# Channel attention of a decoder layer: products of weights and values in two runs of eight per group of heads in place of four runs of four

## The reference, cut to what matters

```python
x = x + _L0_xattn_ref(_layernorm(x, axis=-1), ctx_2048, ctx_2048)   # the stage changed

def _L0_xattn_ref(q, k, v):                  # 8 heads, d = c = 128, m = n = 512
    qh = q.reshape(b * h, d // h, m)
    kh = k.reshape(b * h, d // h, -1)
    vh = v.reshape(b * h, c // h, -1)
    qk = jnp.einsum('bdm,bdn->bmn', qh, kh) * scale
    sm = jax.nn.softmax(qk, axis=-1)
    ret = jnp.einsum('bmn,bcn->bcm', sm, vh)
    return ret.reshape(b, c, m)
```

## Time and profile before

| | |
|---|---|
| median of three runs | 4041.53 us |
| profiled execution | 4037.83 us, span 4036.0 us |
| PE busy | 3624.9 us (90%) |
| DVE busy | 2861.6 us (71%) |
| ACT busy | 2582.2 us (64%) |
| POOL busy | 1597.4 us (40%) |
| mean granted clock of TensorE | 0.972 |
| ring matmuls L336 | 2048 records, 382 ns each |
| max matmuls L354 | 2048 records, 385 ns each |
| pv matmuls L365 | 4096 records, 604 ns each |
| reductions L302 | 1024, 1219 ns each |
| exponentials L380 | 2048, 602 ns each |

### The profile page before, as it was taken

How to read it: one execution, slowest core, us unless ns; L and a number is a source line. 1 busy time by engine, 2 the same in 40 slices (tenths; PEclk the granted TensorE clock), 3 DMA queues, 4 the chain that set the end, 5 groups by cost and what they waited for, 6 DMA issues and landing times. The chain is left out here.

```text
span 4036.0 us, 86194 instructions
## 1 busy us (share of the span) xinstructions
PE 3624.9 (90%) x24451; PEld 1808.3 (45%) x24451; DVE 2861.6 (71%) x4477; ACT 2582.2 (64%) x6419; POOL 1597.4 (40%) x2090
## 2 busy tenths in 40 slices
PE   5999999999999996699999799999976988889896
PEld 1222222222222221577778544444444654655563
DVE  5888888888888885577777577777764455444545
ACT  2777777777777775577777577777762534445353
POOL 6444444444444440666666122222221242332323
PEclk9999999999999998799999999999998999999998
DMA  7777777777777762333333133333323030120202
GB/s 113 125 120 125 120 125 120 125 120 124 120 125 121 123 107 72 103 113 113 112 113 115 58 93 93 93 94 94 94 74 110 1 126 2 64 65 33 95 1 79
DMA packets 342550, 385.82 MB, mean 96 GB/s; under 512 B 58432, under 2 KB 223040, under 8 KB 342336
## 3 DMA queue, kind: packets, MB, share of 16 engines
q1 hardware_dynamic: 315712, 348.69, 40.2%
q10 hardware_dynamic: 26624, 34.63, 3.3%
HBM read 196.52 MB, written 84.93 MB: 70 GB/s over the span
## 5 line engine op out<-in xcount | busy, mean ns | idle before, releaser
L302 DVE TENSOR_REDUCE a_neg_max<-a_max_ps 128x2 f32<-128x1024 f32 x1024 | 1201.3, 1219 | 195.3 <-PE a_max_ps L354 171.2
L380 ACT ACTIVATE a_P<-a_ring_ps 128x512 f32<-128x512 f32 x2048 | 1084.3, 602 | 382.4 <-PE a_ring_ps L336 379.4
L354 PE MATMUL a_max_ps<-a_K,a_Q 96*128 96x512 bf16 x2048 | 621.2, 385 | 44.0 <-DMA a_K<-a_k_split 39.8
L336 PE MATMUL a_ring_ps<-a_Q,a_K 98*128 98x512 bf16 x2048 | 617.6, 382 | 6.3 <-DMA a_Q<-a_max_rows 4.1
L365 PE MATMUL a_pv_ps<-a_P,a_V 128*32 128x512 f32 x4096 | 544.9, 604 | 1.8 <-ACT a_out_sb L385 1.8
L336 PEld LDWEIGHTS a_ring_ps<-a_Q,a_K 98*128 98x128 bf16 x2048 | 159.1, 96 | 660.2 <-ACT a_P L380 585.3
L1163 ACT ACTIVATE c_P<-c_s_ps,c_bias 128x128 f32<-128x128 f32 x1024 | 362.2, 368 | 137.8 <-DVE c_bias L1035 128.6
L1092 PE MATMUL c_s_ps<-c_KD,c_qT 128*128 128x512 f32 x512 | 276.0, 621 | 33.4 <-ACT c_qT L1154 28.9
L1031 DVE TENSOR_REDUCE c_neg_max<-c_s_ps 128x4 f32<-128x512 f32 x256 | 175.5, 686 | 162.2 <-PE c_s_ps L1093 162.2
L354 PEld LDWEIGHTS a_max_ps<-a_K,a_Q 96*128 96x128 bf16 x2048 | 183.1, 98 | 220.7 <-issue 42.5
L256 POOL TENSOR_SCALAR a_var_eps<-a_mean_var 128x1 f32<-128x1 f32 x64 | 12.2, 191 | 648.4 <-DVE a_mean_var L318 648.1
(11 more groups left out here) (250 smaller groups left out, 7245.3 us busy)
## 6 DMA issues: line engine op xcount, KB each, us to landing
a_Q<-a_q_split SPq DMA_DIRECT2D x384, 128.0 KB
a_K<-a_k_split SPq DMA_DIRECT2D x384, 128.0 KB
heads_out<-a_out_sb ACTq DMA_DIRECT2D x128, 256.0 KB, 2.3
a_x_in<-in_x_dram SPq DMA_DIRECT2D x64, 256.0 KB, 3.6
a_c_in<-in_ctx_dram SPq DMA_DIRECT2D x64, 256.0 KB
a_cT_in<-in_ctxT_dram SPq DMA_DIRECT2D x64, 256.0 KB
b_x_in<-in_x_dram SPq DMA_DIRECT2D x64, 256.0 KB, 2.8
b_o_in<-heads_out SPq DMA_DIRECT2D x64, 256.0 KB
```

The costliest lines, as they stand in the source:

```text
L302: dve.tensor_reduce(neg_max[:, p, 2 * u:2 * u + 2], max_ps[u % 2][:, :, :], AX.X, ALU.max, negate=True).then_inc(max_taken, 1)
L336: pe.matmul(ring(s, use_of(k))[:, :], K[i][:, h, n:n + 128], Q[i][:, h, :], start=True, stop=True).then_inc(scores_filled, 1)
L354: last = pe.matmul(max_ps[u % 2][:, j, :], Q[i][0:KROW, h, m:m + 128], K[i][0:KROW, h, :], start=True, stop=True)
L380: act.activation(P[p][k // NT][:, k % NT, :], ring(s, use_of(k))[:, :], ACT.Exp, scale=SCALE).then_inc(exp_done, 1)
```

## The change

In PE's step function the pv matmuls came behind k = 3, 7, 11 and 15, four each time (one position tile t for four heads). Now they come behind k = 7 and k = 15, eight each time (two position tiles). The semaphore `pv_done` still goes up once per position tile. The waits ahead of the first pv matmul of a group (`exp_done`, `v_done`, `out_copied`) move from k = 3 to k = 7. Nothing else is changed.

```diff
-                    if s.exists(-1) and k % NT == NT - 1:
-
-                        g, i, p, t = s.group(-1), s.slot(-1), s.half(-1), k // NT
-                        if t == 0:
+                    if s.exists(-1) and k % 8 == 7:
+
+                        g, i, p = s.group(-1), s.slot(-1), s.half(-1)
+                        if k == 7:
                             pe.wait_ge(exp_done, g * SCORES + SCORES)
                             pe.wait_ge(v_done, s.batch(-1) + 1)
                             at_least(pe, out_copied, g)
-                        for j in range(G):
-                            last = pe.matmul(pv_ps[32 * j:32 * j + 32, :], V[i][:, t, p * G + j, :], P[p][j][:, t, :],
-                                             start=(t == 0), stop=(t == NT - 1))
-                        last.then_inc(pv_done, 1)
+                        for t in range(k // 8 * 2, k // 8 * 2 + 2):
+                            for j in range(G):
+                                last = pe.matmul(pv_ps[32 * j:32 * j + 32, :], V[i][:, t, p * G + j, :], P[p][j][:, t, :],
+                                                 start=(t == 0), stop=(t == NT - 1))
+                            last.then_inc(pv_done, 1)
```

## The result

The changed kernel takes 4108.58 us (median of four runs, 4107.43 to 4110.64), the kernel before in the same comparison 4040.68. The ratio is 1.0168, with a 95% interval of 1.015 to 1.0185: 68 us slower. The forecast was 4118, slower.

A forecast was written before the change was run, and what follows sets the result against it. PE looked like the bound, with DVE close through two shared buffers. Halves of 5.92 and 6.57 us made a 12.49 us group against 11.85; 0.62 x 125 = 77.5 us more gave 4118 us, range 4052 to 4144.

The forecast's parts named there:

- What bounds the kernel: Channel attention: PE busy 1188 of 1200 us looks like the only bound, but it and DVE trade two buffers, neither far ahead.
- the queues: SP and POOL queues: they keep their order, and what they load is groups ahead and gains time.
- (a): PE's pv runs: fewer joints between full and 32-column matmuls, run of 1.90 us, saving 0.19 us per half group.
- the layout: One group's start times laid out by hand: second half 5.92 us, first half 6.57 us.
- (b): Second half: max pairs three and four wait for DVE's reductions, 0.44 us together; the half gets 0.26 us longer.
- (c): First half: ring matmuls k = 4 and 5 wait for ACT's exponentials until 2.56 and 3.04; half of 6.57 us.
- The sum: Whole kernel: group of 12.49 us against 11.85, taken as 0.62 x 125 = 77.5 us more; forecast 4118 us.
- The step from 0.64 to 0.62: Gain in group length: 12.49 - 11.85 = 0.64 us, lowered to 0.62 for six roundings of up to 0.01 each.
- A: Rival for the whole kernel: only PE counts, without waits the joints give 46 us back, 3995 us; chance 5%.
- B: Rival for each half: it gains 0.19 and waits 0.19 us, so the time stays at 4041; chance 4%.
- C: Rival for the first half: DVE's chain holds, ACT's waits don't; 17 us more, 4059; chance 10%.
- D: Rival: the joint inside the run costs 0.10 us and each half slips another 0.1, 4168 us; chance 8%.

The follow-up runs named there:

- e1: Changed kernel with the eight-matmul pv run in the second half only, runs of four behind k = 3 and 7: 4111.7 us, 1.0175 of before.
- e4: Changed kernel's order, each DVE reduction reading half of its elements: 4082.9 us, 1.0103 of before.
- e8: Changed kernel with ACT's output copy L386 moved from behind exponential 1 to ahead of exponential 0: 4082.8 us, 1.0112 of before.
- e7: Changed kernel's order with halved reductions and exponentials, K loads one group later, P prefilled with ones: 3947.8 us, 0.9776 of before.
- e6: Kernel before with halved reductions and exponentials, K loads one group later, P prefilled with ones: 4011.1 us, 0.993 of before.
- e11: Kernel before with max pairs spread, ACT's copy first, transpose behind the first pv run, K loads one group later: 3997.9 us, 0.9891 of before.
- e5: e1 with the six K loads of a batch issued one group later: 4052.1 us, 1.003 of before.
- e2: Changed kernel with the eight-matmul pv run in the first half only, runs of four behind k = 11 and 15: 4145.1 us, 1.0254 of before.

## Why the prediction was right

- **What bounds the kernel.** Right as far as it went: PE's 99% hid that DVE and ACT are each a fraction of a microsecond behind. It missed the fourth party. The DMA of the maxima lands 0.2 us ahead of its use in every second group of the kernel before, and no wait in its table shows that. The prediction put the queues at nothing because their order is kept. That held with 0.6 us to spare in every second group, and that it held was luck: in e1 the same limit cost 60 us.
- **(a) The joints.** The mechanism was right and its size a little low: 0.23 us per half in place of 0.19. The run is 1.86 us, because the first pass of a run takes 0.45 and each later one 0.43; I had given the later ones the first one's time. This is the miss, 2 x 0.04 x 125 = 10 us against 9.5 between 4118 and 4108.6: in the first half too every ring and max pair starts within 0.01 of the layout, and only the run is shorter.
- **(b) Two reductions in series.** Right in every start time of the second half; the wait in the second half is 0.46 us (0.44 forecast), by 5.89 against 5.43. What I left out is that ACT's exponentials set a second limit 0.24 us behind, so a faster DVE gives back only half (e4).
- **(c) ACT in the first half.** Right: ring matmul 4 at 2.55, and e8 shows it by taking the copy out. One start was off without effect: with batch statistics DVE's first reduction comes 1.62 us into the half (832.39 in its timeline; 1.40 forecast), so its second ends at 3.98 and not 3.76, still ahead of the fourth max pair at 4.13.
- **The sum.** 12.40 us per group where I had 12.49 from the layout and 12.47 in the forecast, and 68 us where I had 77.5. The step from 0.64 to 0.62 rests on roundings and not on a row. PE's step function has 131 turns, not 130; the 125 full ones are right.
- **Rivals.** A (joints alone) is what e7 does when the other engines are made light. It was refuted for this kernel by the waits, not by the joints. B (saving and waits cancel) falls with a wait of 0.46 against a saving of 0.23 in the second half. C (ACT's waits not there) falls with ring matmul 4, which starts 0.06 us behind exponential 2, and with e8; D (a joint inside the run) with the 1.86 us. By the drains of the Trainium skill (TensorEngine Tiling, Key Properties) the change should gain, and e6 against e7 agrees with its sign: 63 us for two pairs of mode changes fewer per group, about 0.24 us each. With full reductions and exponentials the waits are larger, and the time moved the other way.

## What to carry to other kernels

PE and DVE share two buffers here and are nearly balanced, and they stay so only while PE's max pairs come at the pace of the reductions. Bunching PE's other work saved real time on PE and turned the slack into waits on both sides. Lay out one period by hand from the rows before such a change: here two reductions in series and three ring buffers gave the time within 0.25%. And look for the transfers that land just in time, because the table of waits does not list them: when only the second half of this change was made, one of them cost 60 of the 70 us.

## What the runs showed of the hardware

- A 32-column bf16 transpose directly behind a run of 32-column float32 matmuls added 0.03 us (e11: it starts 0.88 us behind the start of the run, and the next full-width matmul at 1.03 in place of 1.00). Between full-width matmuls it added 0.25 (e7).
- In the run of 16 records (four passes over the four column strips) of the changed kernel, the passes follow each other at 0.43 us, the time of two plain matmuls of 512 columns, at the clock of 2.4 GHz. Only the first takes 0.45, and the last 0.55 until a full-width matmul starts.
- A DMA of 4 KB took 8.4 us from issue to landing (median of two) when twelve loads of 128 KB had been issued on another queue (e1). With six of them moved one group later the maxima landed 3.4 or 4.9 us behind the first issue (e5), where it was 9.1.
- A DVE instruction on 16 elements per partition took 1.06 us in place of 0.17 and ended 0.03 us behind a POOL instruction that ran beside it (e2, L308 and L279).
